# Three more gate tiles of layer 1 made inside its scans, at step 14 of lanes 7, 8 and 10

## The chip, the cores and the metric

The kernel runs on one core of a Trainium2 chip. The metric is the device time of one launch in microseconds, lower is better. The engines are named as the profile names them: PE (TensorE), DVE (VectorE), ACT (ScalarE), POOL (GpSimd), SP (SyncE, which issues the DMAs).

## The reference

Two layers over an image batch of 4 x 384 x 32 x 32 (1024 positions each). Layer 0 is a four-way selective scan and a small feed-forward. Layer 1 is a Mamba block and a mixture of four experts. What matters here is the Mamba block's input product and gate, cut to:

```python
xz = xs @ in_proj_w.T                  # 384 -> 2 x 768
xin, z = jnp.split(xz, 2, axis=-1)
xin = silu(conv(xin) + conv_b)         # 4 taps over the positions
dt, Bm, Cm = split(xin @ x_proj_w.T)   # rank 24, 16 states, 16 states
h = dA * h + dt * B * xin              # 768 channels x 16 states, over positions
y = (h . C) + xin * D
y = y * silu(z)                        # the gate
out = y @ out_proj_w.T
```

## The kernel before

The 768 channels of the Mamba block are six tiles (f = 0 to 5) of 128 partitions, and the 1024 positions are two halves (c = 0, 1) of 512. So the gate silu(z) is twelve tiles (f, c), each a product of a 384 x 128 piece of in_proj_w with the normalized input `u`, and a Silu.

The images go one after the other. Image 1 makes all gates in its `between_scans` and is not touched. For images 2 to 4 the order is: scans of layer 0, `between_scans` (the feed-forward of layer 0, the norm, the products into layer 1), `fused_scans` for layer 1, `to_experts` or `to_last_experts`.

**between_scans** (lines 1618 to 2025). PE goes through the list `products`, which has for each half the x tile of each f and, if f is in `EARLY_GATES[c]`, its gate tile behind it. Each product is nine matmuls (three pieces of 128 inputs, each in three passes of high and low fp32r parts; lines 1773 to 1775) into one of six PSUM banks. ACT takes an x tile out of its bank (`take`, lines 1860 to 1869), DVE does the other three taps of the convolution (L1989), ACT does its Silu (`silu_x`, L1880) one tile later. A gate tile needs only ACT's Silu (L1875). In the second half two products for the first scan are put between: behind tile (1, 1) that of all six x tiles of the first half with `w1x` (L1811), behind tile (1, 3) that for dt (L1816). After taking tile (1, 4), ACT makes delta's Abs, Exp and Ln (L1926 to L1932), then takes the last tile, whose taps on DVE end the stage. Each stage is a block of its own, and the next begins on every engine when this one is through.

**fused_scans** for layer 1. A lane is one tile f and one half c: lanes 0 to 5 are the first half, lanes 6 to 11 the second. A lane has 16 steps, one for each state n. At each step ACT makes the decay, exp(A delta), in a PSUM bank (`decay`, L1142), POOL makes the drive, du * B (L1227), DVE scans (L1276) and, at two of three steps, multiplies with C (`weigh`, L1285). At n = 1, 4, 7, 10 and 13 the scan goes to SBUF instead and POOL multiplies (L1237). PE adds up the products by transposing them into a bank (`add`, L1007). The scan's order is fixed: each engine goes through its steps in order and waits on semaphores.

The decays take turns in a ring of `SLOTS = 4` banks. The list `places` gives the ring's order: one place a step, and extra places for a projection, delta (step 4), the sum turned back (step 8), an output tile (step 9, lanes 8 to 10) and a gate tile made here ("input", step 9). Place k uses bank 1 + k % 4, and `vacated` makes its first writer wait until the place four before it is free. A step's place is free when it has been multiplied with C (or scanned, when POOL multiplies).

Other work rides along: one pair of hidden units of the experts twice in each lane. Its Gelu (L1173, with a table load in front and one, L1206, behind) is done by ACT after the decay of step 8 and of step 0 of the next lane (`pattern`, whose 16 is that step 0), the up products on PE are at steps 0 and 1, 9 and 10, the down products (L1074) at 11 and 12, and 3 and 4. Delta of the next lane (Abs, Exp, Ln) is made by ACT behind step 5. In lanes 8 to 10 PE makes an output tile at steps 6 and 7 (L1018), and ACT copies it at step 11.

The gate tiles that are not early are made in lanes 0, 1, 2 (half 0, f = 3, 4, 5) and 5, 6, 7 (half 1). SP loads the weights at step 2 (`load_input`, L905) into the one buffer `w_z`, after the tile before is through PE; PE makes three fp32 matmuls at step 6 (`gate_product`, L1041), ACT does the Silu at step 11 (`take_gate`) between two table loads (L1154, L1160). DVE multiplies the first half's gates into y inside the scans (`gate`, L1298); those of the second half are first read in the stage behind the scans.

Of the kernel before, what the change touches and what calls it, by code (L numbers as in the profile page):

```python
# [33 lines left out]
N = 16  # L34
# [9 lines left out]

EARLY_GATES = ((0, 1, 2), (0, 1, 2))
EARLY_COLS = DI + 3 * P

LATE_SILUS = (4, 5)
# [17 lines left out]
def cols(c):  # L66
    return slice(c * HALF, (c + 1) * HALF)
# [591 lines left out]
def fused_scans(p, m, g, st, moved, directions, tiles, rows, guests, pattern, ending, out, following=None, turn=None, load_ahead=None,  # L659
# [47 lines left out]
    product_of = {TILES + 2 + f: f for f in range(CT)} if products is not None else {}  # L707
    INPUT_AT, INPUT_PLACE_AT, INPUT_TAKE_AT = 6, 9, 11
    input_lanes = sorted(inputs.at) if inputs is not None else []
    input_of = {i: k for k, i in enumerate(input_lanes)}  # L710
    input_done = {inputs.at[i]: k + 1 for k, i in enumerate(input_lanes)} if inputs is not None else {}
    TURN_AT, TURN_PLACE_AT, TURN_TAKE_AT = 11, 14, 15
# [90 lines left out]
    places = [("projection", 0), ("delta", 0)]  # L803
    for step in range(STEPS):
        if fresh(step // N + 2) and step % N == PROJECT_AT:
            places.append(("projection", step // N + 2))
        if step // N + 1 < LANES and step % N == DELTA_AT:
            places.append(("delta", step // N + 1))
        if step // N and step % N == SUM_AT:
            places.append(("sum", step // N - 1))  # L810
        if step // N in product_of and step % N == OUT_AT:
            places.append(("out", product_of[step // N]))
        if step // N in input_of and step % N == INPUT_PLACE_AT:
            places.append(("input", input_of[step // N]))
        if step // N in turned_of and step % N == TURN_PLACE_AT:
            places.append(("residual", turned_of[step // N]))
        places.append(("step", step))
# [40 lines left out]
    with nc.Block() as block:  # L858
        @block.sync
        def _(eng):  # L860
# [39 lines left out]
            def load_input(k):  # L900

                f, _ = inputs.at[input_lanes[k]]
                if k:
# [17 lines left out]
            for s in range(LAST + 8):  # L921
                i, n = s // N, s % N
                t = i // TILES
                if s < STEPS:
# [8 lines left out]
                    if guests and s == 5:  # L933
                        load_w2(1)
                    if i in input_of and n == 2:
                        load_input(input_of[i])
                    if late is not None and s == 1:
# [32 lines left out]
        def _(eng):  # L970
# [64 lines left out]
            def gate_product(q):  # L1035

                _, c = inputs.at[input_lanes[q]]
                eng.wait_ge(st.w_input, 16 * (q + 1))
# [39 lines left out]
            for s in range(LAST):  # L1078
# [4 lines left out]
                if s < STEPS:  # L1083
# [6 lines left out]
                    if i in product_of and n in (PRODUCT_AT, PRODUCT_AT + 1):  # L1090
                        product(product_of[i], n - PRODUCT_AT)
                    if i in input_of and n == INPUT_AT:
                        gate_product(input_of[i])
                    if fresh(i + 2) and n in (PROJECT_AT - 3, PROJECT_AT - 2):
# [13 lines left out]
        def _(eng):  # L1108
# [43 lines left out]
            def take_gate(q):  # L1152
                f, c = inputs.at[input_lanes[q]]
                eng.preload_act_table_set(SILU)  # L1154
# [21 lines left out]
            for s in range(LAST):  # L1176
# [3 lines left out]
                if s < STEPS:  # L1180
# [3 lines left out]
                    if i in product_of and n == OUT_COPY_AT:  # L1184
                        copy_out(product_of[i])
                    if i in input_of and n == INPUT_TAKE_AT:
                        take_gate(input_of[i])
                    if i in turned_of and n == TURN_TAKE_AT:
# [1343 lines left out]
def build(nc, io, out, rows, half_rows, normed, gates):  # L2532
    with ExitStack() as ctx:
# [48 lines left out]
        with ExitStack() as conv:  # L2582
# [142 lines left out]
            def shared_scans(name, late, before, following, u_halves, rows_C):  # L2725

                with ExitStack() as scans:
# [16 lines left out]
                    with ExitStack() as ring:  # L2744
                        w_z = tensors(nc, ring, [(f"w_z_{name}", [P, CT, P], F32)])[f"w_z_{name}"]

                        left = [(f, c) for c in range(NH) for f in range(DT1) if f not in EARLY_GATES[c]]
                        inputs = Named(w=w_z, u=u_halves, z=z, silus=[(xin[:, f, cols(1)], m.prod[:, f % 3, cols(1)]) for f in LATE_SILUS], at=dict(zip((0, 1, 2, 5, 6, 7), left)))
                        fused_scans(p, ms, g, s_scan, s_moved, mamba, DT1, half_rows, guests, ((0, 8, 11), (9, 16, 19)),
# [158 lines left out]
```

## Time and profile before

| what | us |
|---|---|
| median of 3 runs | 5680.66 (5675.88 to 5688.37) |
| the profiled execution, its own time | 5684.87 |
| its span | 5683.1 |
| PE, DVE, ACT, POOL busy | 4773.0, 4580.2, 3481.2, 4084.5 |
| mean granted clock of PE | 0.94 |

Shares of the span are averages over stages of quite different make. The times in the rows are us from the start of the span. A timeline row is: start, duration, engine, line, operation, output <- input, how many in a row are merged, and in brackets how long the engine sat idle ahead of it and what ended that.

### The profile page before, as it was taken

The numbers are of one execution on the slowest core, as the hardware profiler recorded it, in microseconds if no ns is written. First come the engines' busy times: TensorE is split into PE (matmuls) and PEld (weight loads), VectorE is DVE, ScalarE is ACT, GpSimd is POOL, SyncE is SP. The second block draws the span as 40 slices with busy tenths as digits, with TensorE's granted clock in tenths as the row PEclk, the third lists the DMA queues.
The fourth block names the chain that finished last, engine by engine and source line by source line (L and its number), as shares of the span: only waits on it lengthen the run. The fifth ranks groups of instructions, "written<-read, shape, count | busy, mean of one in ns | idle before, by whom it ended". The sixth has DMA issues, their size and how long they took to land. (4 is left out here: it accounts for less than half of the span.)

```text
span 5683.1 us, 64490 instructions
## 1 busy us (share of the span) xinstructions
PE 4773.0 (84%) x19309; PEld 3020.2 (53%) x19309; DVE 4580.2 (81%) x4655; ACT 3481.2 (61%) x5292; POOL 4084.5 (72%) x3128
## 2 busy tenths in 40 slices
PE   6787786788989887888998888787989988788998
PEld 2232242236666645555666645555666654556777
DVE  6999947978999948986999966996999985996544
ACT  3444354337878857766888856775878765774221
POOL 6999927958999926875999953994999962984111
PEclk8899998889999999998999999998999999999999
DMA  5666405427778715645787833654778752662110
GB/s 201 231 219 223 164 21 189 153 98 255 268 277 274 259 51 193 221 157 190 270 281 265 280 113 137 220 197 147 265 270 280 259 194 78 205 221 90 43 50 28
DMA packets 341664, 1070.72 MB, mean 188 GB/s; under 512 B 31547, under 2 KB 119463, under 8 KB 334777
## 3 DMA queue, kind: packets, MB, share of 16 engines
q1 hardware_dynamic: 341304, 1066.50, 54.2%
q8 instruction: 157, 2.57, 0.2%
q14 instruction: 203, 1.65, 0.1%
HBM read 1052.69 MB, written 13.68 MB: 188 GB/s over the span
## 5 line engine op out<-in xcount | busy, mean ns | idle before, releaser
L1007 PE MATMUL banks<-ident,prod 128*128 128x128 f32 x4752 | 769.9, 288 | 432.9 <-DVE prod L1285 327.1
L1007 PEld LDWEIGHTS banks<-ident,prod 128*128 128x128 f32 x4752 | 557.9, 145 | 845.2 <-DVE prod L1285 602.9
L455 PE MATMUL banks<-prod,ident 128*128 128x512 f32 x972 | 549.9, 708 | 284.3 <-DVE prod L630 214.9
L1276 DVE TENSOR_TENSOR_SCAN banks<-banks,h 128x512 f32<-128x512 f32 x594 | 723.6, 1218 | 75.5 <-ACT banks L1142 38.3
L1227 POOL TENSOR_TENSOR h<-lane,Bb 128x512 f32<-128x512 f32 x576 | 722.8, 1272 | 56.5 <-DMA Bb<-half_rows 30.5
L1142 ACT ACTIVATE banks<-lane,A 128x512 f32<-128x512 f32 x864 | 580.5, 686 | 258.3 <-DVE prod L1285 88.3
L537 ACT ACTIVATE banks<-delta_first,A 128x1024 f32<-128x1024 f32 x288 | 321.1, 1117 | 517.3 <-DVE prod L630 433.5
L1074 PE MATMUL banks<-w_a,Cb 128*128 128x384 f32 x1536 | 550.5, 487 | 0.0
L455 PEld LDWEIGHTS banks<-prod,ident 128*128 128x128 f32 x972 | 195.9, 217 | 626.3 <-DVE prod L630 359.3
L1276 DVE TENSOR_TENSOR_SCAN banks<-banks,half_carry_a,h 128x512 f32<-128x512 f32 x396 | 505.8, 1277 | 5.8 <-POOL h L1227 3.9
L1227 POOL TENSOR_TENSOR h<-half_du_a,Bb 128x512 f32<-128x512 f32 x384 | 481.8, 1272 | 15.4 <-DMA Bb<-half_rows 11.5
L621 DVE TENSOR_TENSOR_SCAN banks<-banks,h 128x1024 f32<-128x1024 f32 x198 | 453.3, 2289 | 37.2 <-POOL h L586 28.4
L1142 ACT ACTIVATE banks<-half_delta_a,A 128x512 f32<-128x512 f32 x576 | 384.7, 685 | 160.9 <-DVE lane L1257 74.7
L1062 PE MATMUL banks<-big,w_a 128*128 128x256 f32 x1728 | 435.9, 395 | 0.9 <-DMA w_a<-w_in 0.8
L1285 DVE TENSOR_TENSOR prod<-banks,half_C_a 128x512 f32<-128x512 f32 x528 | 365.3, 692 | 75.7 <-DMA half_C_a<-half_rows 4.1
L1227 POOL TENSOR_TENSOR h<-lane,Cb 128x512 f32<-128x512 f32 x288 | 362.9, 1273 | 27.4 <-DVE banks L1276 16.0
L1173 ACT ACT_TABLE_LOAD x288 | 369.5, 1283 | 6.9 <-PE banks L1074 1.9
L1206 ACT ACT_TABLE_LOAD x288 | 369.5, 1283 | 5.0
L586 POOL TENSOR_TENSOR h<-du_first,Cb 128x1024 f32<-128x1024 f32 x144 | 338.1, 2353 | 47.5 <-DVE h L621 22.0
L586 POOL TENSOR_TENSOR h<-du_first,Bb 128x1024 f32<-128x1024 f32 x144 | 345.6, 2410 | 22.8 <-DVE prod L621 12.8
L1062 PEld LDWEIGHTS banks<-big,w_a 128*128 128x128 f32 x1728 | 326.4, 198 | 61.6 <-issue 11.6
L2261 POOL TENSOR_TENSOR w_lo<-raw,w_hi 128x1152 fp32r<-128x1152 f32 x32 | 89.2, 2809 | 352.8 <-ACT w_hi L2341 352.8
(435 smaller groups left out, 11345.3 us busy)
## 6 DMA issues: line engine op xcount, KB each, us to landing
Bb<-half_rows SPq DMA_DIRECT2D x576, 512.0 KB, 4.3
Cb<-half_rows SPq DMA_DIRECT2D x288, 512.0 KB, 4.3
w_a<-w_in SPq DMA_DIRECT2D x256, 576.0 KB, 6.2
Bb<-rows SPq DMA_DIRECT2D x144, 512.0 KB, 4.2
Cb<-rows SPq DMA_DIRECT2D x144, 512.0 KB, 4.0
w_b<-w_in SPq DMA_DIRECT2D x128, 576.0 KB, 6.1
half_C_a<-half_rows SPq DMA_DIRECT2D x128, 512.0 KB, 6.8
C_first<-rows SPq DMA_DIRECT2D x40, 1024.0 KB, 8.2
```

The lines of the kernel that those rows point to most:

```text
L455: mm = eng.matmul(ps[:, c, :], m.ident[:, :], src[:, cols(c)], start=n == 0, stop=added(s) == (i + 1) * N, skip_group_check=True)
L586: eng.tensor_tensor(m.dBu[:, s % DRIVES, :], m.du[:, i % 2, :], m.B[s % BRING], ALU.mult).then_inc(st.dbu, 1)
L621: eng.tensor_tensor_scan(flip(to), flip(slot(s)), flip(m.dBu[:, s % DRIVES, :]), 0.0, ALU.mult, ALU.add).then_inc(st.scanned, 1)
L1007: mm = eng.matmul(ps[:, 0, at], src[:, at], m.ident[:, :], start=n == 0 and k == 0, stop=added(s) == (i + 1) * N, is_transpose=True, skip_ ...
L1062: mm = eng.matmul(hidden(u), g.w1[:, w % WRING, k, t * P:(t + 1) * P], g.un[:, k, at], start=k == 0, stop=k == CT - 1, skip_group_check=True)
L1074: mm = eng.matmul(total(b), g.h[:, u % HRING, b * P:(b + 1) * P], g.w2[:, w % WRING, t, :], start=u % PER == 0, stop=u % PER == PER - 1, s ...
L1142: eng.activation(slot(s), m.delta[i % 2], ACT.Exp, scale=x.A(j, n)).then_inc(st.decay, 1)
L1173: eng.activation(g.h[:, u % HRING, :], hidden(u), ACT.Gelu, bias=m.vec[:, b:b + 1]).then_inc(st.gelu, 1)
L1206: eng.preload_act_table_set(EXP_LN)
L1227: eng.tensor_tensor(m.dBu[:, s % DRIVES, :], m.du[i % 2], m.B[b % BRING][:, cols(s % 2)], ALU.mult).then_inc(st.dbu, 1)
L1276: eng.tensor_tensor_scan(flip(to), flip(slot(s)), flip(m.dBu[:, s % DRIVES, :]), initial, ALU.mult, ALU.add).then_inc(st.scanned, 1)
L1285: eng.tensor_tensor(prods[own(s) % PRODS], slot(s), m.C[:, n, :], ALU.mult).then_inc(st.prod, 1)
```

## The change

The gate tiles 0, 1 and 2 of the second half leave `between_scans`: `EARLY_GATES` has none for c = 1. They are made in `fused_scans` instead. A place for a gate tile is now a pair (lane, step), with the step 9 as before or 14. At 14, SP loads the weights at step 9, PE makes the product at step 11 (after the add, ahead of the down product), the place in the ring is ahead of step 14's, and ACT does the Silu behind the decay of step 15. The nine tiles go in order to (0, 9), (1, 9), (2, 9), (5, 9), (6, 9), (7, 9), (7, 14), (8, 14), (10, 14), so those of the second half are f = 0 to 5 in this order. `EARLY_COLS`, the columns of in_proj_w that `between_scans` loads and splits, stays: the first half's early gates still use them.

```diff
--- before.py
+++ after.py
@@ -42,7 +42,7 @@
 FT = FF // P
 KR = C // RANK
 
-EARLY_GATES = ((0, 1, 2), (0, 1, 2))
+EARLY_GATES = ((0, 1, 2), ())
 EARLY_COLS = DI + 3 * P
 
 LATE_SILUS = (4, 5)
@@ -705,10 +705,12 @@
     GATE_AT, PRODUCT_AT, OUT_AT, OUT_COPY_AT = 9, 6, 9, 11
     gated = range(1, TILES + 1) if products is not None else ()
     product_of = {TILES + 2 + f: f for f in range(CT)} if products is not None else {}
-    INPUT_AT, INPUT_PLACE_AT, INPUT_TAKE_AT = 6, 9, 11
-    input_lanes = sorted(inputs.at) if inputs is not None else []
-    input_of = {i: k for k, i in enumerate(input_lanes)}
-    input_done = {inputs.at[i]: k + 1 for k, i in enumerate(input_lanes)} if inputs is not None else {}
+
+    INPUT_STEPS = {9: (2, 6, 11), 14: (9, 11, 15)}
+    input_places = sorted(inputs.at) if inputs is not None else []
+    input_done = {inputs.at[place]: k + 1 for k, place in enumerate(input_places)} if inputs is not None else {}
+    place_at = {place: k for k, place in enumerate(input_places)}
+    loads, gate_products, silus = ({(i, INPUT_STEPS[n][part]): k for k, (i, n) in enumerate(input_places)} for part in range(3))
     TURN_AT, TURN_PLACE_AT, TURN_TAKE_AT = 11, 14, 15
     turned_of = {i: i for i in range(TT)} if late is not None else {}
     PAIR = QUARTER // P
@@ -810,8 +812,8 @@
             places.append(("sum", step // N - 1))
         if step // N in product_of and step % N == OUT_AT:
             places.append(("out", product_of[step // N]))
-        if step // N in input_of and step % N == INPUT_PLACE_AT:
-            places.append(("input", input_of[step // N]))
+        if (step // N, step % N) in place_at:
+            places.append(("input", place_at[step // N, step % N]))
         if step // N in turned_of and step % N == TURN_PLACE_AT:
             places.append(("residual", turned_of[step // N]))
         places.append(("step", step))
@@ -899,7 +901,7 @@
 
             def load_input(k):
 
-                f, _ = inputs.at[input_lanes[k]]
+                f, _ = inputs.at[input_places[k]]
                 if k:
                     eng.wait_ge(st.input, k)
                 eng.dma_start(inputs.w[:, :, :], p.io["w_in"][:, :, DI + f * P:DI + (f + 1) * P]).then_inc(st.w_input, 16)
@@ -932,8 +934,8 @@
                         load_w1(1)
                     if guests and s == 5:
                         load_w2(1)
-                    if i in input_of and n == 2:
-                        load_input(input_of[i])
+                    if (i, n) in loads:
+                        load_input(loads[i, n])
                     if late is not None and s == 1:
                         eng.wait_ge(st.gates, 16)
                         eng.dma_start(g.turned[:, :], gates.rearrange("o (e l) -> (o e) l", e=E)).then_inc(st.row, 16)
@@ -1034,7 +1036,7 @@
 
             def gate_product(q):
 
-                _, c = inputs.at[input_lanes[q]]
+                _, c = inputs.at[input_places[q]]
                 eng.wait_ge(st.w_input, 16 * (q + 1))
                 vacated(eng, "input", q)
                 for k in range(CT):
@@ -1089,8 +1091,8 @@
                         back(i - 1)
                     if i in product_of and n in (PRODUCT_AT, PRODUCT_AT + 1):
                         product(product_of[i], n - PRODUCT_AT)
-                    if i in input_of and n == INPUT_AT:
-                        gate_product(input_of[i])
+                    if (i, n) in gate_products:
+                        gate_product(gate_products[i, n])
                     if fresh(i + 2) and n in (PROJECT_AT - 3, PROJECT_AT - 2):
                         project(i + 2, n - PROJECT_AT + 3)
                     if i + 1 < LANES and n == DELTA_AT - 4:
@@ -1150,7 +1152,7 @@
                 eng.activation(residual(t), bank("residual", t)[:, 0:C], ACT.Copy).then_inc(st.x_taken, 1)
 
             def take_gate(q):
-                f, c = inputs.at[input_lanes[q]]
+                f, c = inputs.at[input_places[q]]
                 eng.preload_act_table_set(SILU)
                 eng.wait_ge(st.input, q + 1)
                 eng.activation(inputs.z[:, f, cols(c)], bank("input", q), ACT.Silu).then_inc(st.input_taken, 1)
@@ -1183,8 +1185,8 @@
                         copy_sum(i - 1)
                     if i in product_of and n == OUT_COPY_AT:
                         copy_out(product_of[i])
-                    if i in input_of and n == INPUT_TAKE_AT:
-                        take_gate(input_of[i])
+                    if (i, n) in silus:
+                        take_gate(silus[i, n])
                     if i in turned_of and n == TURN_TAKE_AT:
                         take_residual(turned_of[i])
                     if turn is not None and n == 14 and i < TILES:
@@ -2745,7 +2747,7 @@
                         w_z = tensors(nc, ring, [(f"w_z_{name}", [P, CT, P], F32)])[f"w_z_{name}"]
 
                         left = [(f, c) for c in range(NH) for f in range(DT1) if f not in EARLY_GATES[c]]
-                        inputs = Named(w=w_z, u=u_halves, z=z, silus=[(xin[:, f, cols(1)], m.prod[:, f % 3, cols(1)]) for f in LATE_SILUS], at=dict(zip((0, 1, 2, 5, 6, 7), left)))
+                        inputs = Named(w=w_z, u=u_halves, z=z, silus=[(xin[:, f, cols(1)], m.prod[:, f % 3, cols(1)]) for f in LATE_SILUS], at=dict(zip(((0, 9), (1, 9), (2, 9), (5, 9), (6, 9), (7, 9), (7, 14), (8, 14), (10, 14)), left)))
                         fused_scans(p, ms, g, s_scan, s_moved, mamba, DT1, half_rows, guests, ((0, 8, 11), (9, 16, 19)),
                                     ((0, 6, 8), (7, 11, 12)), before,
                                     load_ahead=lambda eng, done: eng.dma_start(w_out[:, :, :], p.io["w_out"]).then_inc(done, 16),
```

## Rows read from the trace of the kernel before

**Rows 1.** The page, part 1: busy us, share of the span, instructions.
```profile
DVE  6999947978999948986999966996999985996544
```

**Rows 2.** Windows, image 2: between_scans, then layer 1's scans; columns as named.
```profile
core 0: us, PE busy (x) PEld busy (x) DVE busy (x) ACT busy (x) POOL busy (x), PEclk, DMA share, GB/s
2025.80:2173.20 147.40, 128.52 (x344) 59.69 (x344) 64.83 (x77) 79.34 (x135) 18.00 (x11) 0.93 0.11 35
2173.20:2543.30 370.10, 296.52 (x1402) 204.27 (x1402) 339.49 (x358) 265.94 (x424) 330.37 (x293) 0.94 0.61 210
```

**Rows 3.** Waits of DVE in lanes 6 to 11: us, times, longest.
```profile
DVE prod L1285 <- DVE banks L1276: 0.5, 1, 0.5
DVE banks L1276 <- POOL h L1227: 0.4, 1, 0.4
```

**Rows 4.** Timeline, PE in between_scans: start, us, engine, line, idle before.
```profile
2146.41 5.36 PE L1811 MATMUL banks<-big,w1x 128*56 128x512 f32 x12 [0.93 <-ACT big L1880]
...
2155.91 0.39 PE L1773 MATMUL banks<-u_hi_a,rows_C_a 128*128 128x512 f32 x1
...
2157.95 0.39 PE L1773 MATMUL banks<-u_hi_a,rows_C_a 128*128 128x512 f32 x1
```

**Rows 5.** Timeline, ACT in the same stage.
```profile
2145.72 0.64 ACT L1880 ACTIVATE big<-prod 128x512 f32<-128x512 f32 x1
...
2163.51 0.60 ACT L1860 ACTIVATE xs_a<-banks 128x512 f32<-128x512 f32 x1 [1.44 <-PE banks L1775]
...
2169.09 0.77 ACT L1869 ACTIVATE prod<-banks,vec 128x512 f32<-128x512 f32 x1
```

**Rows 6.** Timeline, DVE in the same stage.
```profile
2138.88 11.27 DVE L1989 SCALAR_TENSOR_TENSOR prod<-xs_a,vec,prod 128x512 f32<-128x512 f32 x15
...
2169.96 2.91 DVE L1989 SCALAR_TENSOR_TENSOR prod<-xs_a,vec,prod 128x512 f32<-128x512 f32 x3 [0.62 <-ACT prod L1869]
```

**Rows 7.** Windows, PE alone: busy, granted clock, DMA.
```profile
core 0: us, PE busy (x), PEclk, DMA share, GB/s
2114.00:2120.00 6.00, 6.00 (x15) 0.72 0.01 3
```

**Rows 8.** Timeline, PE in the scans, two waits of one length.
```profile
2225.15 1.12 PE L1007 MATMUL banks<-ident,prod 128*128 128x128 f32 x4 [2.65 <-DVE prod L1285]
...
2256.57 0.66 PE L1007 MATMUL banks<-ident,prod 128*128 128x128 f32 x4 [2.65 <-DVE prod L1285]
```

**Rows 9.** Timeline, ACT in lanes 7 to 9.
```profile
2411.00 1.28 ACT L1154 ACT_TABLE_LOAD   x1
...
2414.21 2.52 ACT L1142 ACTIVATE banks<-half_delta_a,A 128x512 f32<-128x512 f32 x4
...
2446.88 0.69 ACT L1142 ACTIVATE banks<-half_delta_a,A 128x512 f32<-128x512 f32 x1 [1.39 <-DVE prod L1285]
2447.59 1.28 ACT L1173 ACT_TABLE_LOAD   x1
...
2451.03 1.92 ACT L1142 ACTIVATE banks<-half_delta_a,A 128x512 f32<-128x512 f32 x3
```

**Rows 10.** Timeline, DVE at the end of lane 8.
```profile
2446.09 0.69 DVE L1285 TENSOR_TENSOR prod<-banks,rows_C_a 128x512 f32<-128x512 f32 x1
...
2451.92 1.28 DVE L1276 TENSOR_TENSOR_SCAN banks<-banks,half_carry_a,h 128x512 f32<-128x512 f32 x1
...
2453.94 1.27 DVE L1276 TENSOR_TENSOR_SCAN h<-banks,half_carry_a,h 128x512 f32<-128x512 f32 x1
```

**Rows 11.** Timeline, all engines, lane 5: a decay and the scan behind it.
```profile
2347.14 1.30 ACT L1142 ACTIVATE banks<-half_delta_a,A 128x512 f32<-128x512 f32 x2
2347.86 1.23 DVE L1276 TENSOR_TENSOR_SCAN banks<-banks,h 128x512 f32<-128x512 f32 x1 [1.25 <-ACT banks L1142]
```

**Rows 12.** Timeline, PE in lanes 7 and 8.
```profile
2407.28 2.74 PE L1041 MATMUL banks<-u_a,w_z_a 128*128 128x512 f32 x6
...
2416.19 1.46 PE L1074 MATMUL banks<-w_a,Cb 128*128 128x384 f32 x4
...
2446.16 1.13 PE L1074 MATMUL banks<-w_a,Cb 128*128 128x384 f32 x3
```

**Rows 13.** One source line, the loads of w_z, from issue to landing.
```profile
DMA to landing us min/median/max: 3.8/5.2/8.7
```

## The prediction

> **What bounds the kernel now.** I read the page's busy times first: VectorE (DVE) is busy 81% of the span [rows 1], but that mean mixes stages, so I went to the windows. The change touches one pair of stages, run three times (images 2 to 4): `between_scans`, 147.4 us, where TensorE (PE) is busy 128.5 us and DVE 64.8, and `fused_scans` of layer 1, 370.1 us, where DVE is busy 339.5 and POOL 330.4 [rows 2]. The first is set largely by PE, the second by DVE. The DVE waits of lanes 6 to 11 (the second half of the positions) make this sharp: in 178 us it waits 0.5 us for itself and 0.4 us for POOL, and never for ScalarE (ACT) [rows 3]. Whatever makes DVE wait there is lost in full. The timelines then show each end of the change.
>
> **What is removed.** In each of the three `between_scans`, the gate products of tiles 0, 1 and 2 of the second half (9 matmuls each) and three Silus of ACT. The order of PE in the second half was x0, g0, x1, then the w1x product, then g1, x2, g2, x3, the dt product, x4, x5.
>
> - g0 lies ahead of the w1x product. That one starts at 2146.41, after 0.93 us of waiting for ACT's `silu_x` of tile 5 (started 2145.72), and this Silu waited in turn for DVE's taps, 15 in a row from 2138.88 for 11.27 us, three to a tile: those of tile 5 are the seventh to ninth, so they end near 2138.88 + 9 x 0.75 = 2145.6 [rows 4, 5, 6]. DVE's taps don't move, so w1x doesn't. g0's 2.04 us and ACT's gate are worth nothing; PE waits some 3.0 us there instead of 0.93.
> - g1 and g2 lie behind it. From w1x to x4, PE doesn't wait. Products start at 2155.91 and 2157.95; the steady step is 2157.95 - 2155.91 = 2.04 us [rows 4]. ACT waits for PE before taking x4, 1.44 us at 2163.51; behind that take hang the table load, Abs, Exp, Ln, the last take (2169.09) and the last taps (2169.96, 2.91 us), and the scans begin [rows 5, 6]. x4 comes 2 x 2.04 = 4.08 us earlier. Would ACT or DVE now bound it? The ACT work between two takes is some 2 us (0.60 + 0.77 and a Silu of 0.64 [rows 5]), the DVE taps of a tile 3 x 0.75 = 2.3 us; x3 comes 2.04 us behind x2 and x4 a dt product later still: both just keep up. I take 4.08 us per image, 12.24 in all, with 0 as the other bound.
> - The clock. With PE waiting 3 us ahead of w1x, its granted clock may fall. The nearest rows disagree: after 2.65 us of waiting, the same four transposes took 1.12 us once (half clock) and 0.66 us once (full) [rows 8]. A fall costs what the one in 2114 to 2120 did: a mean of 0.72 over 6 us, 6 x 0.28 = 1.7 us [rows 7], here on the path. Bounds 0 and 1.7 per image; I take one fall in two, 0.85, or 2.6 us in all.
>
> **What is added** in each layer-1 scan: three more gate tiles, at lanes 7, 8 and 10: a load of w_z (SP, step 9), three fp32 matmuls (PE, step 11, 2.74 us), and on ACT at step 15 a Silu between two table loads, 3.21 us from 2411.00 to 2414.21, as with the tile at step 11 of lane 7 today [rows 9, 12]. The tiles of lanes 5, 6 and 7 at place 9 stay and only have another f. The tiles ahead of all that, in the first half, stay the same.
>
> PE first. In lane 8 the new product fits in where the down product starts now, 2446.16, and ends at 2448.9 [rows 12]. It pushes the adds of steps 12 to 15 back by up to 2.7 us. DVE's product buffers are three deep, so its `weigh` of step 2 of the next lane wants the add of step 14, some 4 us later: no cost.
>
> ACT and the ring of four PSUM banks are where the price is. A place more between steps 13 and 14 shifts the banks of steps 14 and 15 and of step 0 behind them. Step 15's decay now wants the product of step 12 to be out, not that of step 11. Lane 8, worked in its own times:
> 1. DVE ends the product of step 12 at 2446.09 + 0.69 = 2446.78 [rows 10]. Today the decay of step 0 of lane 9 waits for this, starting 2446.88 [rows 9]. Now step 15's starts there.
> 2. Decay 0.71 (2447.59 - 2446.88) to 2447.59; the new excursion 3.21 to 2450.80 (its Silu can start at 2448.9, just when the matmuls end). Step 0's decay to 2451.51: DVE wants it at 2451.92, in time.
> 3. Then the Gelu pair of the hidden units, which ACT does after step 0 in every lane: 2451.03 - 2447.59 = 3.44 us [rows 9], to 2454.95. Only then step 1's decay. DVE can start 0.72 us after it (2347.14 to 2347.86, where it waited for just that) [rows 11]: 2455.67.
> 4. DVE wants step 1 at 2453.94 [rows 10]. It waits 1.73 us.
>
> Two excursions now stand back to back with one decay between them, and that decay was in the banks only because of the look-ahead. DVE has no idle time to pay this from. Lanes 7 and 10 have the same Gelu pair after step 0. So 9 places x 1.73 = 15.6 us. Bounds: 0 (today's excursion at step 11 of lanes 6 and 7 costs DVE nothing [rows 3]) and 3.21 (the whole excursion) per place, 28.9 in all; I take the worked value.
>
> The Trainium skill, page "ScalarE: Activation LUTs", section "What ACT_TABLE_LOAD costs", prices a switch at some 1283 ns of load and 1380 ns of drain. By that page each place would be longer by 2 x 1.38 us, and nine by 24.8 us. The trace agrees with the load (1.28 us) and not with the drain: the load at 2447.59 begins where the decay started at 2446.88 ends, 0.69 us later [rows 9].
>
> SP: the load at step 9 of lane 7 must wait until the product made at step 6 of the same lane is through PE (2407.28 + 2.74 = 2410.0), as w_z has one buffer. The next load on the queue is that of B at step 11, so little is held up behind it. It lands 5.2 us later in the median, 3.8 to 8.7 [rows 13]: 2415.2, for a product at 2416.19 [rows 12]. In lanes 8 and 10 the buffer has long been free.
>
> **Sum.** -12.2 + 2.6 + 15.6 = +6.0 us (rounded). The profiled execution took 5684.87 us (span 5683.1), so it would be 5690.9; the median of the runs is 4.2 us lower, 5680.66, and gives 5686.7. What can be told from no change here is 0.2%, 11.4 us.
>
> **Rivals.**
> - *The wait isn't there* (faster, on the other side). ACT gets through to step 1 in time. For this: today's excursions in lanes 6 and 7 are free. Against: three steps lie between them and the Gelu pair. Time: 5680.66 - 12.2 + 2.6 = 5671.0, or 5668.4 if the clock doesn't fall. The sum turns negative when a place costs less than 9.6 / 9 = 1.07 us; it is faster by more than 0.2% only near zero. Chance 0.06.
> - *The weights of lane 7 come late.* The product is wanted at 2416.19, so w_z must land within 6.2 us of its issue at 2410.0. At the 8.7 us that one load took, ACT's Silu, and DVE behind it, are another 2.5 us late in each image: 5686.7 + 7.5 = 5694.2. It decides from about 7.9 us on (11.4 - 6.0 = 5.4 us over three images, 1.8 each). Chance 0.10.
> - *The change doesn't shorten `between_scans`*: ACT or DVE takes PE's place after w1x. For: DVE's taps of 2.3 us are close to the 2.04 us step. Against: today ACT waits for PE, and DVE for ACT, in each turn there. 5680.66 + 15.6 = 5696.3, slower by 0.28%. Chance 0.06.
> - *The drain is there after all*: +6.0 + 24.8 gives 5711.5. The page's rule; the row speaks against it. Chance 0.02.
> - My forecast, between 5679 and 5694 by a place's cost of 1.0 to 2.4 us and zero to three falls of the clock: 0.76.
>
> **How the numbers follow.** The low end reaches half way to the first rival, 5674; the high end takes in the late weights and the lost gain, 5698. Slower by over 0.2% (above 5692): the two rivals above it, the drain, and the top of my own range: 0.18. Faster by over 0.2% (below 5669.3): 0.03. Else 0.79.
>
> **What would show it.** In the profile after: the last tap of `between_scans` ends 4.1 us (or 2.4) sooner after the w1x product starts, PE waits some 3 us ahead of w1x and DVE waits for ACT once, 1.7 us, before the scan of step 1 of lanes 8, 9 and 11, where it waits for nothing today. I am wrong if that wait stands elsewhere (step 0, or PE's product is late and ACT sits idle before the Silu), or if the scans' 370 us grow by less than 3 or more than 8 us per image.

## The result, and the profile after

The change makes the kernel a little slower: 5693.08 us in the median (5689.0 to 5703.54) against 5682.95 for the kernel before on the same chip (5673.44 to 5692.89), 17 runs each. The ratio is 1.0019 [1.0012, 1.0025], so +0.19%, about 10 us. That is only just within the 0.2% that I had called no change, and the interval reaches 0.25%. I had forecast +6.0 us, 0.11%, which is below the interval. The profiled executions differ by 5696.2 - 5683.1 = 13.1 us of span.

One thing to put right ahead of it: the row under [rows 1] is DVE's line of the 40 slices, not its busy time. The busy time, 4580.2 us (81%), stands in the table. After the change the page's part 1 reads:

```profile
PE 4787.6 (84%) x19282; PEld 3026.1 (53%) x19282; DVE 4582.2 (80%) x4655; ACT 3506.4 (62%) x5310; POOL 4088.5 (72%) x3128
```

DVE has the work it had, ACT 25 us more (23 of them for 18 more table loads of 1.28 us), and PE 15 us more: 6 of them since a gate tile takes 2.74 us in the scans and took 2.04 before, the rest where its clock is lower. The page can't say where 13 us went. Lines of the kernel have numbers that are two higher than before (the scan is L1278, the decay L1144, the multiplication with C L1287, the w1x product L1813).

Windows of image 2, `between_scans` and the scans of layer 1, with the columns of [rows 2]. The first two rows are before, the last two after, cut at the same instructions: DVE's first one of the stage, its first scan, and its first one behind the scans.

```profile
2030.90:2175.17 144.27, 123.46 (x338) 57.42 (x336) 64.83 (x77) 80.01 (x136) 19.22 (x12) 0.94 0.10 32
2175.17:2543.49 368.32, 296.68 (x1402) 204.27 (x1402) 339.49 (x358) 263.98 (x422) 328.44 (x292) 0.94 0.61 211
...
2027.82:2169.10 141.28, 118.35 (x311) 51.99 (x309) 64.73 (x77) 78.64 (x133) 19.82 (x12) 0.92 0.11 33
2169.10:2544.74 375.64, 307.81 (x1420) 211.12 (x1420) 340.49 (x358) 273.19 (x431) 328.88 (x292) 0.93 0.60 208
```

(In [rows 2] the first window begins 5.1 us earlier and ends 2.0 us ahead of the first scan.) DVE is busy 64.73 and 340.49 us instead of 64.83 and 339.49. What changed is its waiting. To have the whole account I measured each image's two stages in both traces in this way, the second one cut where the first scan of lane 6 starts:

| us, images 2 / 3 / 4 | before | after | difference, sum of three |
|---|---|---|---|
| between_scans | 144.27 / 144.03 / 143.48 | 141.28 / 141.77 / 142.08 | -6.7 |
| scans, first half | 186.39 / 186.93 / 186.42 | 188.35 / 187.90 / 187.07 | +3.6 |
| scans, second half | 181.93 / 181.94 / 181.58 | 187.29 / 187.27 / 188.45 | +17.6 |

That is +14.5, and the stages elsewhere gave 1.4 back. Now the ends. The timeline of PE, the w1x product of images 2, 3 and 4 ([rows 4] has image 2 of before: 5.36 us, behind 0.93 us of waiting):

```profile
2142.95 6.80 PE L1813 MATMUL banks<-big,w1x 128*56 128x512 f32 x12 [2.98 <-ACT big L1882]
...
3467.01 6.96 PE L1813 MATMUL banks<-big,w1x 128*56 128x512 f32 x12 [3.00 <-ACT big L1882]
...
4787.90 6.99 PE L1813 MATMUL banks<-big,w1x 128*56 128x512 f32 x12 [3.00 <-ACT big L1882]
```

PE waits 3.0 us, and the same twelve matmuls then take 6.80 to 6.99 us instead of 5.36. Windows over them in images 2 and 4 (0.76 in image 3 too), PE alone, with the granted clock as third figure from the end (columns as in [rows 7]):

```profile
2142.95:2149.68 6.73, 6.73 (x12) 0.78 0.00 0
...
4787.90:4794.82 6.92, 6.92 (x12) 0.76 0.01 2
```

A mean of 0.76 to 0.78 is a stretch that is partly at 1.2 GHz and partly at 2.4. The end of the stage, from the timelines of ACT and DVE ([rows 5, 6] have before):

```profile
2157.43 0.60 ACT L1862 ACTIVATE xs_a<-banks 128x512 f32<-128x512 f32 x1 [0.90 <-PE banks L1777]
...
2163.89 2.91 DVE L1991 SCALAR_TENSOR_TENSOR prod<-xs_a,vec,prod 128x512 f32<-128x512 f32 x3 [0.63 <-ACT prod L1871]
```

From the start of w1x to the last taps it was 2169.96 - 2146.41 = 23.55 us, and is 2163.89 - 2142.95 = 20.94 us.

In the scans, DVE's timeline of image 2 shows the new waits for ACT, in front of step 1 of lanes 8, 9 and 11. The last row is of before:

```profile
2422.12 1.28 DVE L1278 TENSOR_TENSOR_SCAN h<-banks,half_carry_a,h 128x512 f32<-128x512 f32 x1 [1.58 <-ACT banks L1144]
...
2453.37 1.28 DVE L1278 TENSOR_TENSOR_SCAN h<-banks,half_carry_a,h 128x512 f32<-128x512 f32 x1 [1.76 <-ACT banks L1144]
...
2456.32 0.69 DVE L1287 TENSOR_TENSOR prod<-banks,rows_C_a 128x512 f32<-128x512 f32 x1 [0.48 <-PE banks L1009]
...
2515.35 1.28 DVE L1278 TENSOR_TENSOR_SCAN h<-banks,half_carry_a,h 128x512 f32<-128x512 f32 x1 [1.70 <-ACT banks L1144]
...
2456.88 0.69 DVE L1285 TENSOR_TENSOR prod<-banks,rows_C_a 128x512 f32<-128x512 f32 x1 [0.48 <-DVE banks L1276]
```

The wait of 0.48 us, in front of the multiplication of step 2 of lane 9, isn't new: before, DVE waited 0.48 us at the same instruction in images 2 and 3, and not in image 4, and so it is after. Only the releaser that the profile names is another. So in images 2 and 3 the three waits for ACT are the whole growth: 5.04 us of idle time in each, and some 0.3 us more since the 5.36 and 5.33 us of the table also hold the overlap that DVE loses at a wait (without one, a scan starts 0.08 us before the multiplication ahead of it ends).

And ACT's timeline at the border of lanes 8 and 9 ([rows 9] has before) shows why:

```profile
2444.40 0.69 ACT L1144 ACTIVATE banks<-lane,A 128x512 f32<-128x512 f32 x1 [1.33 <-DVE prod L1287]
2445.11 1.28 ACT L1156 ACT_TABLE_LOAD   x1
2446.57 0.60 ACT L1158 ACTIVATE big<-banks 128x512 f32<-128x512 f32 x1 [0.18 <-PE banks L1043]
2447.19 1.28 ACT L1162 ACT_TABLE_LOAD   x1
2448.49 0.69 ACT L1144 ACTIVATE banks<-half_delta_a,A 128x512 f32<-128x512 f32 x1
2449.20 1.28 ACT L1175 ACT_TABLE_LOAD   x1
2450.49 0.84 ACT L1175 ACTIVATE Cb<-banks,vec 128x256 f32<-128x256 f32 x2
2451.35 1.28 ACT L1208 ACT_TABLE_LOAD   x1
```

Read it from the top: step 15's decay, which had to wait for DVE; the gate's excursion; step 0's decay; the Gelu pair's excursion, ending at 2452.63. Step 1's decay starts at 2452.65 and DVE at 2453.37, 0.72 us later. Two excursions with one decay between them: from 2445.09 to 2452.65, 7.6 us, ACT makes a single decay, where DVE takes one about every 2 us.

In image 4 the same border of lanes costs more, and PE is in it. ACT's timeline in lane 8, then DVE's:

```profile
5085.03 0.60 ACT L1148 ACTIVATE big<-banks 128x512 f32<-128x512 f32 x1 [3.23 <-PE banks L1020]
...
5091.95 0.60 ACT L1158 ACTIVATE big<-banks 128x512 f32<-128x512 f32 x1 [1.41 <-PE banks L1043]
```

```profile
5094.59 1.29 DVE L1278 TENSOR_TENSOR_SCAN banks<-banks,half_carry_b,h 128x512 f32<-128x512 f32 x1 [0.85 <-ACT banks L1144]
...
5098.74 1.28 DVE L1278 TENSOR_TENSOR_SCAN h<-banks,half_carry_b,h 128x512 f32<-128x512 f32 x1 [2.04 <-ACT banks L1144]
```

The copy of the output tile waited 3.23 us for its product (L1020; 1.70 in images 2 and 3, 1.65 before), then the gate's Silu 1.41 us for the gate product (0.18 in images 2 and 3): PE is behind. DVE waits 0.85 us at step 0 and then 2.04 at step 1, where it was 1.76 in image 2; with 0.20 us earlier in the lane that is 1.3 us more, and the second half grew by 1.5 us more.

What differs between the images is PE's clock. Windows of PE in images 2 and 4 (image 3 has 0.91 as well), from 60 to 80 us behind the first scan of lane 6, so around the start of lane 8:

```profile
2417.45:2437.45 20.00, 17.25 (x77) 0.91 0.63 210
...
5061.31:5081.31 20.00, 17.26 (x73) 0.83 0.65 216
```

A mean of 0.83 over 20 us is 3.4 us lost, one of 0.91 is 1.8 us. The three images have the same work there, and PE's longest wait is 2.27 us in each.

### The profile page after: what moved, and what is told of

It is laid out like the page before. It is cut to its first block and busy times, and to the rows that moved or that the text cites. A ratio compares the mean times of both kernels' runs of the same rounds, so it can differ in the third digit from the quotient of the medians.

```text
span 5696.2 us, 64472 instructions
## 1 busy us (share of the span) xinstructions
PE 4787.6 (84%) x19282; PEld 3026.1 (53%) x19282; DVE 4582.2 (80%) x4655; ACT 3506.4 (62%) x5310; POOL 4088.5 (72%) x3128
## 3 DMA queue, kind: packets, MB, share of 16 engines
q14 instruction: 202, 1.65, 0.1%
## 5 line engine op out<-in xcount | busy, mean ns | idle before, releaser
L1278 DVE TENSOR_TENSOR_SCAN banks<-banks,h 128x512 f32<-128x512 f32 x594 | 723.7, 1218 | 77.9 <-POOL h L1229 38.6
L1144 ACT ACTIVATE banks<-lane,A 128x512 f32<-128x512 f32 x864 | 580.9, 687 | 258.6 <-DVE prod L1287 94.4
L1076 PE MATMUL banks<-w_a,Cb 128*128 128x384 f32 x1536 | 550.8, 487 | 0.0
L1278 DVE TENSOR_TENSOR_SCAN banks<-banks,half_carry_a,h 128x512 f32<-128x512 f32 x396 | 506.0, 1278 | 5.8 <-POOL h L1229 4.0
L1229 POOL TENSOR_TENSOR h<-half_du_a,Bb 128x512 f32<-128x512 f32 x384 | 482.3, 1274 | 14.5 <-DMA Bb<-half_rows 9.9
L1144 ACT ACTIVATE banks<-half_delta_a,A 128x512 f32<-128x512 f32 x576 | 384.8, 686 | 148.6 <-DVE lane L1259 73.2
L1287 DVE TENSOR_TENSOR prod<-banks,half_C_a 128x512 f32<-128x512 f32 x528 | 365.4, 692 | 75.2 <-DMA half_C_a<-half_rows 3.4
L1175 ACT ACT_TABLE_LOAD x288 | 369.5, 1283 | 6.9 <-PE banks L1076 1.9
L1208 ACT ACT_TABLE_LOAD x288 | 369.5, 1283 | 5.1
```

What stands on the lines that cost most here:

```text
L1076: mm = eng.matmul(total(b), g.h[:, u % HRING, b * P:(b + 1) * P], g.w2[:, w % WRING, t, :], start=u % PER == 0, stop=u % PER == PER - 1, s ...
L1144: eng.activation(slot(s), m.delta[i % 2], ACT.Exp, scale=x.A(j, n)).then_inc(st.decay, 1)
L1175: eng.activation(g.h[:, u % HRING, :], hidden(u), ACT.Gelu, bias=m.vec[:, b:b + 1]).then_inc(st.gelu, 1)
L1208: eng.preload_act_table_set(EXP_LN)
L1229: eng.tensor_tensor(m.dBu[:, s % DRIVES, :], m.du[i % 2], m.B[b % BRING][:, cols(s % 2)], ALU.mult).then_inc(st.dbu, 1)
L1278: eng.tensor_tensor_scan(flip(to), flip(slot(s)), flip(m.dBu[:, s % DRIVES, :]), initial, ALU.mult, ALU.add).then_inc(st.scanned, 1)
```

## The experiments

Eight kernels: the first four on one chip, on which the kernel before took 5681.21 us, the other four on a second one, where it took 5682.16. So each is compared with its own kernel before, and the change itself with the +10.1 of its own measurement. The ratio to the kernel before stands behind each time, with its interval. Where the interval holds 1 (keep_g0, lane_11, gelu_17, and take_14 at its edge), the medians tell no difference, and the argument goes by the waits in the traces. The theory was the one on record: nine waits of some 1.7 us behind two excursions, less what `between_scans` gives back, which is cut by a falling clock. The rivals were that PE's added work is the cost, that the place in the ring alone is (whatever ACT does there), and that the clock doesn't matter.

**add_only**: the three tiles are made twice, early as before and in the scans too.

```diff
-EARLY_GATES = ((0, 1, 2), ())
+EARLY_GATES = ((0, 1, 2), (0, 1, 2))
-left = [(f, c) for c in range(NH) for f in range(DT1) if f not in EARLY_GATES[c]]
+left = [(f, c) for c in range(NH) for f in (3, 4, 5)] + [(0, 1), (1, 1), (2, 1)]
```

> All gate tiles are still made in between_scans, and (0, 1), (1, 1), (2, 1) are made a second time at step 14 of lanes 7, 8 and 10. Theory (two table excursions back to back after step 15 make DVE wait at step 1 of the next lane): between_scans as before, 144 us from its first DVE instruction to the first scan; DVE waits for ACT 1.6 to 1.8 us at nine places, and the time is 15 to 16 us over the kernel before. Rival (the excess of the change comes from elsewhere, such as a late start of the scans' loads): the scans grow by 7 us per image or more here too with the stage ahead unchanged, 21 us, or by less than 3.

Measured: 5702.26 us, 1.0033 [1.0021, 1.0045], +21: my number was missed, and it is the one that I had given to the rival. The scans grew by 7.9, 5.0 and 8.0 us per image, so two images went the rival's way and one the theory's. `between_scans` is as before (144.12 / 142.90 / 144.04, w1x 5.36 us behind 0.98 us). The second half grows by 6.9 / 5.3 / 6.9 us. Waits of DVE there, in image 2:

```profile
DVE h L1278 <- ACT banks L1144: 5.3, 3, 2.0
DVE banks L1278 <- ACT banks L1144: 1.1, 2, 0.9
DVE prod L1287 <- PE banks L1009: 0.5, 1, 0.5
```

The first row holds the three waits at step 1, 1.58, 2.04 and 1.70 us, where 5.0 us in all was to be expected. The 0.3 above that and the second row, 1.4 us together, I had costed at nothing; the third row is the 0.48 us that were there before. The 1.4 us stand in lane 8 and at its border with lane 9, as in image 4 of the change: ACT waits 3.30 us for the output product there and 1.42 for the gate product. PE's clock over the same 20 us, in images 2, 3 and 4:

```profile
2427.03:2447.03 20.00, 17.26 (x73) 0.83 0.63 212
3748.87:3768.87 20.00, 15.99 (x77) 1.00 0.64 212
5069.12:5089.12 20.00, 17.26 (x73) 0.83 0.67 209
```

In image 3, with PE at its full clock, the three waits for ACT are 1.59, 1.70 and 1.69 us and nothing else is added: 5.3 us of growth, as the theory has it, with the gate product of 2.74 us in lanes 7, 8 and 10 all the same. So 15.9 of the 19.1 us of growth are the theory's, and the rest is what the lower clock of PE in images 2 and 4 costs.

**remove_only**: the three tiles are left out early and not made at all.

```diff
-left = [(f, c) for c in range(NH) for f in range(DT1) if f not in EARLY_GATES[c]]
+left = [(f, c) for c in range(NH) for f in (3, 4, 5)]
```

> The three gate tiles are left out of between_scans and made nowhere (the gate is then what the tile held before). Theory: w1x starts when it did, PE waits 3.0 us ahead of it, its clock falls each time and w1x takes 6.8 to 7.0 us in place of 5.4; what is left of 4.08 us is 2.4 to 2.6 per image, and the time is 7 to 8 us under the kernel before. Rival (the clock's fall is a matter of this one profile): w1x takes 5.4 us in some images, and the time is 10 to 12 us under it. Second rival (the first half's scans suffer from the earlier start, 0.7 to 2 us per image in the profile of the change): the time is only 3 to 5 us under it, with longer waits of DVE in lanes 0 to 5.

Measured: 5671.76 us, 0.9986 [0.9977, 0.9995], -9.5 by the medians. The second half is as before (181.97 / 181.97 / 181.61), so everything that it lost under the change came with the three places. PE waits 3.0 us ahead of w1x in all three images. In images 2 and 3 it then goes like this:

```profile
2143.89 6.89 PE L1813 MATMUL banks<-big,w1x 128*56 128x512 f32 x12 [2.99 <-ACT big L1882]
...
3455.91 5.36 PE L1813 MATMUL banks<-big,w1x 128*56 128x512 f32 x12 [3.00 <-ACT big L1882]
```

The same wait, and once the clock falls, once it doesn't; in image 4 it falls. I had expected a fall each time, and 7 to 8 us. From the start of w1x to the last taps it is 21.04 and 19.47 us, against 23.55 before: -2.5 with a fall, -4.08 without.

**copy_14**: at the three new places ACT copies the bank instead of doing a Silu, so there is no table load.

```diff
+                if input_places[q][1] == 14:
+                    eng.wait_ge(st.input, q + 1)
+                    eng.activation(inputs.z[:, f, cols(c)], bank("input", q), ACT.Copy).then_inc(st.input_taken, 1)
+                    return
                 eng.preload_act_table_set(SILU)
```

> The change, but the three tiles at step 14 are taken with a Copy that needs no table, so without the six table loads per image (these gates lack their Silu). Bank, matmuls, load and the order of the steps stay. Theory (the table loads, 2.6 us a place, are what makes step 1's decay late): no wait of DVE at step 1 of lanes 8, 9 and 11, and the time is that of remove_only, 7 to 8 us under the kernel before, within 2 us. Rival (the place in the ring or PE's product makes ACT late): waits of 0.5 us or more stay there, and the time is at or above the kernel before.

Measured: 5675.44 us, 0.999 [0.9981, 0.9999], -5.8. The second half costs 0.8 / 0.8 / 0.9 us more than before, not 5 to 7. ACT at the same border of lanes, image 2:

```profile
2444.35 0.69 ACT L1144 ACTIVATE banks<-lane,A 128x512 f32<-128x512 f32 x1 [1.33 <-DVE prod L1291]
2446.46 0.60 ACT L1158 ACTIVATE big<-banks 128x512 f32<-128x512 f32 x1 [1.42 <-PE banks L1043]
2446.95 0.69 ACT L1144 ACTIVATE banks<-half_delta_a,A 128x512 f32<-128x512 f32 x1
2447.66 1.28 ACT L1179 ACT_TABLE_LOAD   x1
```

The place in the ring and PE's product are there, and ACT even idles 1.42 us for that product. From the start of step 15's decay to that of step 0's it is 2.60 us, where it was 4.09 with the table loads (2444.40 to 2448.49), and DVE waits some 0.3 us at step 1 twice, instead of 1.7 three times. So the place in the ring and the product, even together, cost 0.8 us per image at most; the rest is the excursion. I had expected no wait at all and the time of remove_only within 2 us; it is 3.7 us above that, of which these 2.5 us are a part.

**keep_g0**: the tile ahead of w1x stays early, so only lanes 7 and 8 have a place at step 14.

```diff
-EARLY_GATES = ((0, 1, 2), ())
+EARLY_GATES = ((0, 1, 2), (0,))
-..., (7, 9), (7, 14), (8, 14), (10, 14)
+..., (7, 9), (7, 14), (8, 14)
```

> Gate tile (0, 1) stays in between_scans, where it stood ahead of w1x and cost nothing; only (1, 1) and (2, 1) move, to step 14 of lanes 7 and 8. Theory: PE waits 0.9 us ahead of w1x, the clock stays, between_scans is 4.1 us shorter per image; six waits of 1.7 us cost 10.2; the time is 12.2 - 10.2 = 2 us under the kernel before, and 12 us under the change. Rival (the fall of the clock has nothing to do with the wait ahead of w1x): w1x takes 6.8 to 7.0 us here too and the time is 2 to 3 us over the kernel before.

Measured: 5684.4 us, 1.0005 [0.9996, 1.0014], +3.2: my number was missed, by 5 us. The rival's number came, but not its reason, as w1x keeps its speed in all three images. `between_scans` did what I said, 140.03 / 140.23 / 139.93:

```profile
2146.28 5.36 PE L1813 MATMUL banks<-big,w1x 128*56 128x512 f32 x12 [0.97 <-ACT big L1882]
```

That is -4.2 / -3.8 / -3.6, with one tile more made early than under the change. But the second half grew by 4.9 / 5.2 / 5.2 us with two places, where 2 x 1.73 was expected. DVE's waits there:

```profile
DVE h L1278 <- ACT banks L1144: 3.3, 2, 1.8
DVE late_xt L1312 <- PE banks L1076: 1.2, 1, 1.2
DVE prod L1287 <- PE banks L1009: 0.5, 1, 0.5
```

The first row is the 2 x 1.7, and the last one was there before. What is left is DVE waiting 1.22 us for a down product of PE (L1076) early in lane 9. Image 4 has the same, 1.56 us; in both the granted clock around the start of lane 9 is low, 0.84 from 90 to 112 us behind the first scan of lane 6, where it is 0.92 in image 3. Image 3 has instead the waits of lane 8 that image 4 of the change has, 1.4 us together, with a clock of 0.83 there.

The next four kernels ask where the work would be cheap. **lane_11**: one tile early, the other two at lanes 10 and 11, where no other lane, and no Gelu pair, follows the second.

```diff
-EARLY_GATES = ((0, 1, 2), ())
+EARLY_GATES = ((0, 1, 2), (0,))
-..., (7, 9), (7, 14), (8, 14), (10, 14)
+..., (7, 9), (10, 14), (11, 14)
```

> As keep_g0, but the two moved tiles are at step 14 of lanes 10 and 11. Lane 11 is the last: no Gelu pair and no lane stands behind its Silu, and ACT waits 7 us for its last sum. Theory (the cost is two excursions back to back ahead of step 1's decay): one wait of 1.7 us per image, in lane 11; the last sum of lane 11 at most 1 us later; 5 to 8 of the 12.2 us gained are lost no more, so the time is 5 to 7 us under the kernel before and 8 us under keep_g0. The extra waits that PE's backlog brings in lanes 8 and 9 are gone. Rival (each tile costs its PE and ACT time wherever it stands): as keep_g0, 2 to 3 us over the kernel before.

Measured: 5676.95 us, 0.9993 [0.9984, 1.0002], -5.2, as expected. The second half grows by 1.8 us in each image, DVE waits once:

```profile
DVE h L1278 <- ACT banks L1144: 1.7, 1, 1.7
```

and in lane 11 ACT has its excursion, then idle time (its timeline):

```profile
2531.51 1.28 ACT L1156 ACT_TABLE_LOAD   x1
2532.81 0.60 ACT L1158 ACTIVATE big<-banks 128x512 f32<-128x512 f32 x1
2533.42 1.28 ACT L1162 ACT_TABLE_LOAD   x1
2537.18 0.60 ACT L1168 ACTIVATE prod<-banks 128x512 f32<-128x512 f32 x1 [2.47 <-PE banks L1009]
```

One excursion costs 1.7 us or nothing, by what follows it; in lane 11 neither a Gelu pair nor another decay does. Against keep_g0 it also does without lane 8, and the waits for PE are gone.

**take_14**: the change, with the gate product a step sooner and the Silu behind step 14's decay, so that two decays stand between the excursions.

```diff
-    INPUT_STEPS = {9: (2, 6, 11), 14: (9, 11, 15)}
+    INPUT_STEPS = {9: (2, 6, 11), 14: (9, 10, 14)}
```

> The change, with the tile's product at step 10 and its Silu behind the decay of step 14, ahead of that of step 15. Theory: ACT is idle there for 1 to 2 us, as step 15's decay waits for the product of step 12; the excursion begins before that wait and not after it, so step 1's decay is 1.1 us earlier: waits of 0.6 to 0.8 us in place of 1.7, and the time is 8 to 10 us under the change, within 3 us of the kernel before. Rival (the place in the ring costs, wherever the Silu is): waits of 1.7 us stay and the time is that of the change.

Measured: 5678.7 us, 0.9991 [0.9982, 1.0], -3.5, so some 14 us under the change, more than I had expected. The second half grows by 3.4 / 1.6 / 3.3 us instead of 5.4 / 5.3 / 6.9. DVE's waits there, image 2:

```profile
DVE banks L1278 <- POOL h L1229: 1.6, 2, 1.1
DVE h L1278 <- ACT banks L1144: 1.4, 3, 0.6
```

The three waits for ACT at step 1 together are 1.4 us (0.19, 0.63 and 0.57), not 5.04. New in the first row is one late drive of POOL, 1.15 us, in lane 8 (0.42 us of the row were there before). It stands in images 2 and 4, where PE's clock around the start of lane 8 is 0.83, and not in image 3, where it is 0.91 and the growth 1.6 us.

**gelu_17**: the change, with the Gelu pair behind step 1's decay instead of step 0's, in every lane.

```diff
-((0, 8, 11), (9, 16, 19))
+((0, 8, 11), (9, 17, 19))
```

> The change, with the second Gelu pair of each lane one step later, behind the decay of step 1 of the next lane. Theory: DVE no longer waits at step 1, but at step 2, which it reaches 1.2 us later while ACT has one decay of 0.7 us more ahead of it: waits of 1.2 us in place of 1.7; the time is 3 to 5 us under the change. Rival (PE or the ring sets the wait): waits of 1.7 us, at step 1 still, and no gain.

Measured: 5687.28 us, 1.0006 [0.9997, 1.0015], +5.1, so 5 us under the change, as expected. The wait moves and shrinks: now it stands at step 2. At step 1, which now has the gate's excursion ahead of it and no Gelu pair, DVE waits for nothing. This is the plainest sign that it takes both.

```profile
DVE banks L1278 <- ACT banks L1144: 3.3, 3, 1.1
```

Its image 2 is the second stage in which w1x kept its speed behind a long wait: 5.36 us from 2148.39, behind 3.00 us.

**all_three**: lane_11, take_14 and gelu_17 together.

> lane_11, take_14 and gelu_17 together: gate (0, 1) stays in between_scans, the two moved tiles at lanes 10 and 11, product at step 10, Silu behind step 14's decay, Gelu pair behind step 1's. Theory: no wait over 0.3 us of DVE for ACT in lanes 6 to 11, all of 12.2 us kept: 10 to 12 us under the kernel before. Rival (the later Gelu pair pushes PE's down products and the sums): 3 us or more of it lost again in either half.

Measured: 5672.08 us, 0.9984 [0.9975, 0.9993], -10.1, as expected. It is faster than the kernel before by 0.16%, clear of the noise, and than the change by some 0.35% (by way of the two measurements of the kernel before). `between_scans` is 139.93 / 140.25 / 139.78, w1x takes 5.36 us in all images, the second half grows by 0.5 us, and of the waits for ACT one of 0.27 us is left; the other two rows were there before the change [rows 3]:

```profile
DVE prod L1287 <- DVE banks L1278: 0.5, 1, 0.5
DVE banks L1278 <- POOL h L1229: 0.4, 1, 0.4
DVE banks L1278 <- ACT banks L1144: 0.3, 1, 0.3
```

## Why the prediction was right, and where its terms were off

**g0 is worth nothing, w1x waits 3.0 us.** Right: 2.98, 3.00 and 3.00 us.

**g1 and g2 give 4.08 us per image.** Right where the clock holds: 23.55 - 19.47 = 4.08 us from w1x to the last taps (remove_only, image 3), and 2.4 to 2.6 with a fall. ACT and DVE keep up, as I had taken. The rival that the stage isn't shortened is out.

**The clock, taken at one fall in two of 1.7 us.** The size was about right: w1x took 1.44, 1.60 and 1.63 us more under the change, where 1.7 was taken. The frequency was not. In the five kernels without g0 (the change, remove_only, copy_14, take_14, gelu_17) the clock fell in 13 of 15 stages behind a wait of some 3.0 us. In the other kernels, before among them, it fell in none of 15 behind some 0.97 us. The term was 2.6 us and came to three falls, 4.7 us. The two stages without a fall had a higher clock in the 60 us ahead of w1x too, 1.00 and 0.97, where the thirteen others had 0.94. Windows of remove_only, PE alone, the 60 us ahead of w1x in images 2 and 3:

```profile
2083.89:2143.89 60.00, 55.74 (x165) 0.94 0.00 0
...
3395.91:3455.91 60.00, 55.76 (x170) 1.00 0.00 0
```

Image 3 did there in 60 us what takes image 2 some 3.6 us more (60 x 0.06), and its whole stage was 136.17 us against 141.48; the other 1.6 us are w1x. So a stage's length varies by a few us with the clock alone, and I judge this stage by the distance from w1x to the last taps and not by its whole length.

**Nine waits of 1.73 us.** Right in place, mechanism and size: 1.58, 1.76 and 1.70 in image 2, 5.04 us for three, where 5.2 was worked out. With the overlap lost at each it is some 1.8 us a place, 16.1 for nine. copy_14 shows that the excursion makes them, and the others that it takes the second excursion behind it: with one more decay between them the three waits are 1.4 us (take_14), with the pair one step later there is none at step 1 and 3.3 us for three at step 2 (gelu_17), with both none in lane 10 (all_three), and none where neither follows (lane_11, in lane 11).

**PE's backlog "no cost".** Right for the work that the prediction looked at, and incomplete. Where PE's clock holds, 2.74 us more of PE cost DVE nothing (add_only, image 3), and nothing in images 2 and 3 of the change either. What the prediction left out is that PE's clock falls in the scans too, around the start of lane 8, and that the backlog adds to this. Once it does so before the change as well (0.91 in image 2). These are the 18 second halves with gate tiles at step 14 of lanes 7 and 8 (the change, add_only, copy_14, keep_g0, take_14, gelu_17), by PE's clock from 60 to 80 us behind the first scan of lane 6:

| second halves | PE's clock there | DVE waits more, us |
|---|---|---|
| six: the change 4, add_only 2 and 4, keep_g0 3, take_14 2 and 4 | 0.83 | 1.3 to 1.5 |
| two: keep_g0 2 and 4 | 0.91, and 0.84 from 90 to 112 us | 1.2 and 1.6, in lane 9 |
| ten: the rest | 0.91 or 1.00 | none; 0.5 in gelu_17, image 3 |

(The number behind a kernel is the image.) The first six, and no others, have ACT waiting 3.2 to 3.3 us for the output product of lane 8. In the 12 second halves without these tiles (before, remove_only, lane_11, all_three) the clock there is never below 0.91. For the change it comes to 1.5 us, all in image 4, where also, as I had named for a sign of being wrong, ACT sits idle 1.41 us before the Silu.

**The first half stays the same.** In this profile it did not: +3.6 us, in code that is the same. DVE waits more there for POOL, 0.5 to 0.9 us per image, and once 1.2 us for a DMA. The three first halves together are 559.7 us before and 563.3 after, and 560.6 to 562.3 in the eight other kernels (561.5 in add_only, which is the kernel before up to lane 7). So the profile before is the lowest of ten and that of the change the highest, and much of the 3.6 us is scatter; whether the change adds to it stays open, and no experiment was made on it.

**The sum.** Forecast +6.0: -9.6, +15.6. Measured in the profile: -6.7 + 17.6 + 3.6 - 1.4 = +13.1, and +10.1 between the medians. The scans grew by 7.3, 6.3 and 7.5 us per image, inside the 3 to 8 that I had named. By terms, of the 7.1 us between forecast and profile, the clock at w1x is 2.1 us, the waits for ACT 0.5, the backlog with the lower clock 1.5, the first half 3.6, what else changed in `between_scans` 0.9, and the stages elsewhere -1.4. The three falls at w1x, where one and a half were taken, and the clock in lane 8 are the part with a cause; that the rest is small is in part luck.

**The other rivals.** The loads of w_z land after 2.7 / 4.2 / 9.4 us (least, median, most), and lane 7's gate is in time; the late weights did not come. The drain isn't there. By the Trainium skill, page "ScalarE: Activation LUTs", section "What ACT_TABLE_LOAD costs", a switch has 1380 ns of drain besides its 1283 ns of load. The trace agrees with the load and not with the drain. The load at 2445.11 stands 0.02 us behind the end of the decay, 2444.40 + 0.69, and the Gelu starts at 2450.49, 0.01 us behind its load.

What stays open: why PE's clock falls by more in lane 8 of one image than of another, behind the same wait of 2.27 us (0.91, 0.91 and 0.83 under the change, 0.83, 1.00 and 0.83 in add_only), and what is left of the 3.6 us of the first halves.

## What to carry to other kernels

When work moves under an engine that waits for nothing, its price is not its length but what stands behind it on the engine that takes it: one 3.2 us excursion of ACT cost DVE 1.7 us a step ahead of another excursion, 0.2 to 0.6 us with a second decay between them, and nothing where none followed. Write out that engine's order for two steps past the new work before choosing the place. And look at what the removed work kept busy: a product that was worth nothing on the critical path kept PE's wait at 1 us instead of 3 and so, in all stages seen, its clock up, and moving it brought nothing: from w1x to the last taps it is 4.1 us shorter with it left in place, and mostly 2.4 to 2.6 without it. A backlog that is covered at full clock may not be at the clock that PE is granted: read that of the stretch, image by image, before calling it free.

## What the runs showed of the hardware

- Behind a wait of PE of some 3.0 us the granted clock fell in 13 of 15 cases, behind some 0.97 us in none of 15. A fall made 5.36 us of matmuls 6.80 to 7.04 us long (under the change at a mean clock of 0.76 to 0.78). I had expected one in two, from two waits of 2.65 us that went different ways [rows 8].
- The clock also moves elsewhere for no cause that I can name: 60 us of one stage ran at 1.00 in one image and at 0.94 in another of the same execution.
- Around the start of lane 8, behind a wait of PE of 2.27 us, the mean clock over 20 us was 0.83, 0.91 or 1.00 from image to image of the change and of add_only. The 3.4 us lost at 0.83 made DVE wait 1.3 to 1.5 us, the 1.8 us lost at 0.91 nothing.
- Two table loads with a 512-wide Silu between them took ACT 3.21 us before [rows 9] and 3.19 in lane_11, and 0.18 us more where the Silu waited for its product; gaps of 0.01 to 0.02 us stood on either side.
